# Second cross attention, selection stage: the next batch's keys projected in two halves, four chunks in the old batch's last step and four in the new batch's first

## The reference, cut to what matters

```python
Q = (x_text @ Wq).reshape(Bb, Tt, H, DH)            # H = 4 heads of DH = 32
K = (x_vision @ Wk).reshape(Bb, Gg, H, DH)          # 4096 keys
scores = jnp.einsum('bthd,bghd->bhtg', Q, K) / np.sqrt(DH)
scores = jnp.where(vision_mask[:, None, None, :], scores, -jnp.inf)
topv, topi = jax.lax.top_k(scores, K_TOP)           # K_TOP = 32
probs = jax.nn.softmax(topv, axis=-1)
attn = jnp.zeros_like(scores).at[bi, hi, ti, topi].set(probs)
attn_mean = attn.mean(axis=1)                       # mean over the heads
c_t = einsum(attn_mean, x_vision @ Wv)              # the context product
```

## Time and profile before

| | us |
|---|---|
| median of 3 runs | 2303.34 |
| profiled execution, its own time | 2318.84 |
| span of its trace | 2317.0 |
| TensorE busy (share of the span) | 1866.9 (81%) |
| VectorE busy | 1237.4 (53%) |
| ScalarE busy | 1026.6 (44%) |
| GpSimd busy | 746.1 (32%) |

### The profile page before, as it was taken

One profiled execution on the slowest core, in us unless ns is written; L12 is line 12 of the kernel. 1 busy time (PEld: TensorE's weight loads), 2 busy tenths in 40 slices (PEclk: granted clock), 3 DMA queues, 4 the chain that ended last, 5 costly groups with the idle time before them and its releaser, 6 DMA issues.

```text
span 2317.0 us, 34831 instructions
## 1 busy us (share of the span) xinstructions
PE 1866.9 (81%) x13676; PEld 1137.7 (49%) x13676; DVE 1237.4 (53%) x3075; ACT 1026.6 (44%) x1381; POOL 746.1 (32%) x665
## 2 busy tenths in 40 slices
PE   5879998999999998886778787786868657976675
PEld 2434544454455445564565244454544445765553
DVE  5142332424232202635882768979868956536575
ACT  1357567656756782221311434545444420113452
POOL 6244234414333400000200356777748601110000
PEclk7989999999999998999787556687776778988887
DMA  6656457664655520001100021221311322000000
GB/s 139 127 101 122 100 122 120 118 128 93 121 111 111 85 70 1 2 1 60 61 1 13 1 62 39 61 79 44 92 49 48 103 72 108 1 1 1 1 5 14
DMA packets 78046, 150.01 MB, mean 65 GB/s; under 512 B 15464, under 2 KB 63144, under 8 KB 71464
## 3 DMA queue, kind: packets, MB, share of 16 engines
q1 hardware_dynamic: 64304, 101.80, 15.7%
q0 software_dynamic: 12768, 42.59, 12.1%
q10 hardware_dynamic: 792, 3.17, 0.4%
HBM read 93.59 MB, written 2.62 MB: 42 GB/s over the span
## 4 chain that ended last, share of the span: by engine, by line
PE 52%; DVE 22%; ACT 12%; issue 6%; POOL 4%; DMA 3%; DVEq 0%; ACTq 0%; POOLq 0%; SPq 0%
PE R L112 33%; PE B L112 17%; ACT P L571 7%; DVE PM L1700 5%; DVE CA L1658 4%; PE B L178 2%; POOL KST L789 2%; ACT PM L1585 2%; DVE CA L1670 1%; DVE T L1672 1%; ACT PS L2266 1%; DMA KST<-OV 1%; POOL ACC L1773 1%; ACT RT L116 1%; DMA CT<-in_ctxT 1%
## 5 line engine op out<-in xcount | busy, mean ns | idle before, releaser
L571 ACT ACTIVATE P<-R 128x1024 f32<-128x1024 f32 x512 | 507.1, 1026 | 220.8 <-PE R L112 185.0
L112 PE MATMUL R<-QS,KST 100*128 100x256 bf16 x2048 | 297.5, 277 | 63.7 <-ACT P L571 53.2
L112 PEld LDWEIGHTS R<-QS,KST 100*128 100x128 bf16 x2048 | 170.5, 98 | 228.3 <-ACT P L571 121.0
L116 ACT ACTIVATE SC<-R 128x1024 f32<-128x1024 f32 x128 | 129.5, 1023 | 256.4 <-PE R L112 143.5
L1658 DVE MAX8 CA<-SC 128x8 f32<-128x128 f32 x1024 | 203.2, 276 | 15.7 <-ACT SC L116 14.8
L200 POOL TENSOR_TENSOR LNrs<-LNve,pk_const 128x2 f32<-128x2 f32 x36 | 25.3, 703 | 535.2 <-DVE LNve L196 535.0
L112 PE MATMUL R<-OV,QT 32*128 32x512 f32 x512 | 197.3, 860 | 0.0
L1773 POOL TENSOR_TENSOR ACC<-ACC,PM 128x4096 f32<-128x4096 f32 x21 | 186.1, 8862 | 1.8
L1700 DVE SCALAR_TENSOR_TENSOR PM<-SC,T,PM 128x4096 f32<-128x4096 f32 x32 | 147.9, 4658 | 50.8 <-ACT AT L116 33.3
L789 POOL DMA_DIRECT2D KST<-OV x300 | 144.5, 490 | 70.8 <-PE R L112 53.9
L112 PE MATMUL R<-P,VP 128*32 128x256 f32 x2304 | 155.9, 387 | 0.7 <-ACT P L571 0.3
(11 more groups left out here) (360 smaller groups left out, 3356.9 us busy)
## 6 DMA issues: line engine op xcount, KB each, us to landing
KST<-OV POOLq DMA_DIRECT2D x276, 128.0 KB, 11.1
CT<-in_ctxP SPq DMA_DIRECT2D x40, 768.0 KB, 4.9
CN<-in_ctxn SPq DMA_DIRECT2D x64, 384.0 KB, 3.3
CT<-in_ctxT SPq DMA_DIRECT2D x64, 192.0 KB, 2.4
KST<-OV SPq DMA_DIRECT2D x84, 128.0 KB, 10.2
KST<-in_ctxP ACTq DMA_DIRECT2D x4, 768.0 KB, 9.5
QS<-x_q POOLq DMA_DIRECT2D x24, 128.0 KB, 5.4
pk_a<-in_pk_a SPq DMA_DIRECT2D x1, 3014.0 KB, 16.9
```

Source lines behind the costliest of these rows:

```text
L112: return e.matmul(o, l, r, start=st, stop=sp, skip_group_check=True)
L116: return e.activation(o, i, ACT.Copy)
L571: e.activation(P[(32 * p + k0) % 3][:, :], ring.at(("s", p, k0))[:, :], ACT.Exp).then_inc(*EX.up((p, k0)))
```

## The change

`rekey(n)` goes and `rekeyed(n, ch)` comes. Key chunks 0 to 3 of the next batch are projected in steps 3, 7 and 11, behind the score chunks 1, 3, 5 and 7. Key chunks 4 to 7 are projected in steps 4, 8 and 12, ahead of the score chunks 0, 2, 4 and 6 of the new batch. ScalarE copies each in the same place of its order, and SP issues each chunk's two loads there: those of chunks 4 to 7 come behind `mask_rows` and the first two `context_in`. Nothing else is added or removed.

```diff
-            def rekey(n):
-                return n // 4 + 1 if n % 4 == 3 and n // 4 + 1 < NB else None
+            def rekeyed(n, ch):
+                if n % 4 == 3 and ch % 2 == 1 and n // 4 + 1 < NB:
+                    return n // 4 + 1, ch // 2
+                if n % 4 == 0 and ch % 2 == 0 and 0 < n < NP:
+                    return n // 4, 4 + ch // 2
+                return None
...
                     for ch in range(8):
+                        if n % 4 == 0 and rekeyed(n, ch):
+                            keys["tensor"](e, *rekeyed(n, ch))
                         if n < NP:
                             scores(n, ch)
-                        if kb_ is not None:
-                            keys["tensor"](e, kb_, ch)
+                        if n % 4 == 3 and rekeyed(n, ch):
+                            keys["tensor"](e, *rekeyed(n, ch))
...
                     for ch in range(8):
+                        if n % 4 == 0 and rekeyed(n, ch):
+                            keys["scalar"](e, *rekeyed(n, ch))
                         if n < NP:
                             copy(n, ch)
...
-                        if kb_ is not None and ch % 2 == 1:
-                            keys["scalar"](e, kb_, ch - 1)
-                            keys["scalar"](e, kb_, ch)
+                        if n % 4 == 3 and rekeyed(n, ch):
+                            keys["scalar"](e, *rekeyed(n, ch))
...
                     for ch in range(8):
-                        if rekey(n) is not None:
-                            keys["sync"](e, rekey(n), ch)
+                        if rekeyed(n, ch):
+                            keys["sync"](e, *rekeyed(n, ch))
```

More of the change, by code:

```diff
@@ L1549, in tensor @@
                         flag(n - 2)
-                    nb_, kb_ = query(n), rekey(n)
+                    nb_ = query(n)
                     m, gs = context(n)
```

## The result

The changed kernel took 2292.14 us (median of 10 runs, 2282.86 to 2298.08), the kernel before 2304.37 (10 runs). The ratio is 0.9936, with a 95% interval of 0.9918 to 0.9955: 15 us less (the medians alone differ by 12). Forecast were 2280 and a range of 2266 to 2299.

The account below looks back on a forecast made before the run. The selection stage's step rhythm was taken to bound the kernel, with selects waiting for ScalarE and TensorE where keys are projected. Gains 30.4 minus losses 7.2 gave 23.2 us: 2303.3 to 2280.1, own range 2270 to 2290, 8-in-10 range 2266 to 2299.

Parts of the forecast that it names:

- the rule of the intervals: Selection step: interval = 8.9 + W + 8.2 us (8.5 in step 7), unless VectorE's own work, some 32.5, is longer.
- rival 1: One of steps 4, 8, 12 stays at 1.2 GHz to its end: 2290 to 2294 us; chance 0.14.
- Steps 3, 7, 11: Steps losing key chunks 4 to 7: gains of 11.1, 8.5 and 10.8 us, together 30.4.
- late tokens: Step 7, same sum for step 11: 0.8 us waiting for key chunk 2's loads, queued behind a context load on SP.
- the slow start of the scores: Step 7, from score chunk 2: before the clock rises, the first 2.7 us do the work of 1.3.
- Steps 4, 8, 12: Steps receiving four key chunks, two of them inside W: losses of 3, 3.9 and 0.3 us, together 7.2.
- keys 5: Key chunk 5, ahead of score chunk 2: in step 8 it ends some 5 us behind the selects.
- The wait ahead of key chunk 4 in step 4: TensorE waiting for key chunk 4's loads: at most 1 us, under cover of the waits for the selects.
- W: Time from the end of a pair's selects to the end of ScalarE's last score or key copy of the step.
- The rest of a context step is as before.: Context steps, apart from the moved key work: unchanged, costed at nothing.
- 2: Rival: steps 4, 8, 12 at 1.2 GHz become the bound, losses 45.9 against gains 30.4; 2319 us, chance 0.09.
- 3: Rival: TensorE granted 2.4 GHz throughout, step 3 too, another 10.6 us there, no losses; 2262 us, chance 0.06.

Follow-up runs that it names:

- e3_loads_again: Changed kernel with each key chunk's two loads issued on SP at the place of the chunk before it; ratio 0.9899 to the kernel before.
- e1_first_half: Changed kernel without key chunks 4 to 7 of batches 1 to 3, which altered the data and the branches taken; 2835.39 us.
- e2_no_keys: Changed kernel without any key chunks of batches 1 to 3, which altered the data and the branches taken; 2423.16 us.
- e5_all_in_new: Changed kernel with all 8 key chunks of a batch in steps 4, 8 and 12, none in steps 3, 7 and 11; 2363.03 us, ratio 1.0229.
- e3_loads_first: First run of the program of e3_loads_again: changed kernel with each key chunk's loads issued one chunk's place earlier on SP; ratio 0.9861.
- e8_double_old: Changed kernel with the matmuls of key chunks 0 to 3 done twice in steps 3, 7 and 11; 2295.27 us, ratio 0.9930.
- e6_filler: Changed kernel with six unused 128x128 fp32 matmuls behind each odd score chunk of steps 2 and 3; ratio 0.9954.
- e4_two_ahead: Changed kernel with key chunk 1 directly behind key chunk 0 in steps 3, 7 and 11; 2301.00 us, ratio 0.9946.

## Why the forecast was right, and where it was off

The direction, the place and the rule of the intervals hold. The number is less good than it looks: 2292.1 lies inside the range of 2266 to 2299 but outside the forecast's own 2270 to 2290. It falls where rival 1 was put (2290 to 2294), and yet none of steps 4, 8 and 12 stayed at 1.2 GHz to its end. Worked through by its own steps:

- **Steps 3, 7, 11: 30.4 us were to go.** Means of two profiles each: 54.6 to 43.2, 46.9 to 39.1, 47.1 to 41.3, that is 11.4 + 7.8 + 5.8 = 25.0. Step 3 (11.1) is right. Steps 7 and 11 fell short of 8.5 and 10.8. One mis-sized term is the late tokens, 2.3 and 3.1 us instead of 0.8 each in the first profile: key chunk 1's loads too stand behind a context load on SP, and I had counted key chunk 2's alone. The other is the clock, which I kept up from its rise to the end of the step. It fell again: some 1.7 us in key chunk 2 of step 7 and its product, 2.8 in key chunk 1 of step 11 and its product, and in step 11 of the second profile all from score chunk 2 to key chunk 1 ran at 1.2 GHz behind a wait of 7.67 us. Against that, the slow start of the scores (1.4 us) did not come; they ran at 2.4 GHz from score chunk 2 on in three of the four steps. `e3_loads_again` has no waits for tokens, and 34.8 and 34.5 there. Of step 11's shortfall of 5.0, 1.2 is the kernel before, whose own step took 48.3 and 45.8.
- **Steps 4, 8, 12: 7.2 us were to come.** Measured 0 in step 4 (clock up at 1391), 3.8 in step 8 (37.0 against 33.2), and step 12 0.8 less than before (34.6 against 35.4): 3.0. The first transposes' wait for GpSimd is where step 8's forecast put it, but keys 5 did not end 5 us behind the selects; they ended 2 us ahead of them, and the loss came from the scores behind the wait, at 1.2 GHz. The size was right for a wrong reason: 3.9 was forecast for a late key chunk 5, and this came by luck near the 3.8 that the slow scores cost. The wait ahead of key chunk 4 in step 4 was 2.07 us and not at most 1, but still under cover: score chunk 2 began 1.1 us behind the selects, as in step 3. (In the recorded sum for step 4 the terms give W 18.8, not 19.2, and the interval before gives 15.8, not 16.2; the loss of 3 is the same.)
- **The six steps together**: 22.1 us gained (250.0 to 227.9), forecast 23.2.
- **"The rest of a context step is as before."** The sum has no term for the nine steps that the change does not touch, and this is the step that failed. The others took 306.9 us before and 314.7 after (means of two), 7.8 more, and 22.1 - 7.8 = 14.3 is near the gain that was timed (15 and 14 us). That agreement is partly luck: taken one by one, the first profiles differ by 22.6 us over the fifteen steps and the second by 6.0. Nothing in the nine steps was changed. Where they are long, the clock is low; windows of the changed kernel over the intervals of steps 9, 13 and 14 (columns as in the earlier trace rows):

```profile
1558.00:1591.00 33.00, 23.22 (x90) 14.05 (x90) 30.60 (x101) 17.92 (x16) 27.79 (x6) 0.71 0.17 49
...
1700.00:1738.00 38.00, 25.42 (x92) 16.08 (x93) 30.78 (x102) 17.61 (x16) 30.31 (x6) 0.63 0.15 42
1738.00:1775.00 37.00, 30.85 (x111) 17.47 (x110) 30.41 (x101) 17.21 (x15) 21.45 (x5) 0.64 0.14 43
```

VectorE does 30.4 to 30.8 us of work in each, and the step is 4 to 5 us longer at 0.63 than at 0.71. The other runs bear this out. In eleven profiles (all but `e1_first_half`, `e2_no_keys` and `e5_all_in_new`), steps 5, 6, 9, 10 and 13 to 16 make 88 intervals. The 21 of 37 us or more had a granted clock of 0.54 to 0.64, the 60 of less than 35.2 one of 0.65 to 0.77, the seven between them 0.64 to 0.74. How it lengthens a step is seen in the changed kernel's second profile: in step 13 (39.3 us) TensorE waits 6.81 us for the selects and then does the scores from chunk 2 to chunk 7 at 1.2 GHz, which is what rival 1 feared for steps 4, 8 and 12. What decides where the clock is low is open. The same program of `e3_loads_first` had 306 and 322 us in the nine steps, and `e8_double_old`, which has the change too, 305.4. So the change does not force them to be longer; whether it makes them so on the mean, two profiles of either kernel can't show. What is shown is that they vary by as much as the whole gain, and that in these profiles they took back a third of what the six steps gave.

The rivals: none of steps 4, 8 and 12 stayed at 1.2 GHz to its end in the two profiles (1 and 2). Step 3 did not rise (3), though in `e8_double_old` it did. The page that I held against the trace, the Trainium skill's TensorE: Matmul & The Clock Gate, Part 1, says that sustained activity releases the throttle. The trace of before disagreed in step 3 (0.50 at 31.1 of 33 us busy). In `e6_filler` and `e8_double_old` the clock did rise within that step.

The fastest versions are the change with earlier loads, without fillers in step 3 (0.9861 and 0.9899) and with them (0.9867 and 0.9870).

## What to carry to other kernels

Price moved work by where it lands against the one wait that ends last: a chunk beside that wait cost its step nothing, the same chunk behind it cost 3.3 us of its 3.7 (`e4_two_ahead`). Then look at the next step, which gave those 3.3 us back. Follow the moved work's loads through their issue queue as well: here the kernels with another order of loads were 0.4 to 0.8% faster, beside the move's 0.6. And where TensorE alternates between work and waits, let the range include the granted clock of the steps that the change does not touch.

## What the runs showed of the hardware

- A busy TensorE can stay at 1.2 GHz: step 3, with matmuls over 1, 32 and 96 rows, did so in both profiles of before (0.50 granted while busy 31.1 of 33 us), and in both of the changed kernel. Doubling four of its key chunks (`e8_double_old`) brought the clock up within the step (0.76 granted), which took 39.9 us instead of 43.2; 24 unused 128-row matmuls did the same (0.78 and 0.77) and made it 5 to 6 us shorter. The rows alone do not decide, as `e8_double_old` added 96-row matmuls only, nor does their number alone: the kernel before had as many of them in this step, in eight strings rather than four, and stayed at 0.50. What does is open.
- One program's executions differ by 29 us (`e3_loads_again`: 2275.16 to 2304.35). Of the 29 between its two profiles (2304.45 in `e3_loads_first`, 2275.16), 15.6 lie in the nine steps that project no keys.
